# Decoder layer on one core: x1 turned by DVE instead of PE in the attending stage

## The reference

```python
x = _layernorm(x + _L0_attn_ref(x, L0_attn_w_qkv, L0_attn_w_out), axis=-1)
x = _layernorm(x + _L0_xattn_ref(x, ctx_1024, ctx_1024, mask, W_q, b_q, W_k, b_k, W_v, b_v, W_o, b_o), axis=-1)
x = _layernorm(x + _L0_ffn_ref(x, kernel, bias, a, b), axis=-1)
```

```python
q, k, v = split(queries @ W_q + b_q), split(keys @ W_k + b_k), split(values @ W_v + b_v)
scores = where(mask == 0, -1e6, einsum('bhqd,bhkd->bhqk', q, k) / sqrt(32))
out = einsum('bhqk,bhkd->bhqd', softmax(scores), v) @ W_o + b_o
```

## Time and profile before

| | us |
|---|---|
| runs | 956.74, 960.45, 960.53 |
| median | 960.45 |
| profiled execution | 956.11 |
| its span, first to last instruction | 954.3 |
| granted TensorE clock, mean over the span | 0.978 |

### The profile page before, as it was taken

How to read it: one execution, slowest core, us unless ns; L and a number is a source line. 1 busy time by engine, 2 the same in 40 slices (tenths; PEclk the granted TensorE clock), 3 DMA queues, 4 the chain that set the end, 5 groups by cost and what they waited for, 6 DMA issues and landing times.

```text
span 954.3 us, 14493 instructions
## 1 busy us (share of the span) xinstructions
PE 903.3 (95%) x4348; PEld 741.0 (78%) x4348; DVE 675.6 (71%) x1132; ACT 378.1 (40%) x1403; POOL 375.7 (39%) x338
## 2 busy tenths in 40 slices
PE   4897999999999999999779999999999999999997
PEld 4783887888888888888678788888888888888775
DVE  3364466666666657466668988979889798887967
ACT  3152221201020211101386656746467565675711
POOL 2000364334343534314237454344544354433733
PEclk9997999999999999999879999999999999999999
DMA  5965430415325120103513032220322204120021
GB/s 181 317 162 90 97 78 34 100 55 78 75 57 86 56 78 22 67 23 124 176 41 99 22 93 64 81 75 22 99 55 90 66 20 125 29 90 20 17 78 45
DMA packets 134172, 76.03 MB, mean 80 GB/s; under 512 B 104488, under 2 KB 106792, under 8 KB 134128
## 3 DMA queue, kind: packets, MB, share of 16 engines
q1 hardware_dynamic: 134127, 75.49, 29.4%
HBM read 52.60 MB, written 22.87 MB: 79 GB/s over the span
## 4 chain that ended last, share of the span: by engine, by line
PE 40%; DVE 5%; issue 2%; ACT 2%; POOL 2%; DVEq 0%; POOLq 0%
PE shared_ps L85 30%; PE score_ps L85 4%; PE shared_ps L1164 4%; ACT probs L1370 1%; DVE score_ps L1676 1%; PE shared_ps L1197 1%; PE shared_ps L1127 1%; POOL probs L1519 1%; DVE xT_lo L1633 1%; DVE x_and_res L1722 1%; DVE stats L1706 0%; DVE pT_lo L1660 0%; DVE top_s L1681 0%; DVE y L1700 0%; POOL x_and_res L1534 0%
## 5 line engine op out<-in xcount | busy, mean ns | idle before, releaser
L1370 ACT ACTIVATE probs<-score_ps,top_s 128x77 f32<-128x77 f32 x512 | 159.0, 359 | 37.7 <-DVE top_s L1681 37.4
L1370 ACT ACTIVATION_READ_ACCUMULATOR probs<-score_ps,top_s 128x1 f32 x512 | 123.1, 241 | 0.0
L1519 POOL TENSOR_TENSOR probs<-probs,per_total 128x616 f32<-128x616 f32 x64 | 82.7, 1308 | 66.0 <-DVE per_total L1688 65.8
L1512 POOL TENSOR_TENSOR rstd<-ve,half_power 128x1 f32<-128x1 f32 x64 | 42.3, 661 | 155.9 <-DVE ve L1711 151.4
L1676 DVE COPY_PREDICATED score_ps<-hidden,masked 128x616 f32<-128x616 int32 x64 | 66.6, 1040 | 11.3 <-PE score_ps L85 11.2
L1377 ACT ACTIVATE pT_hi<-shared_ps 103x512 fp32r<-103x512 f32 (+1 forms) x96 | 54.8, 612 | 44.0 <-PE shared_ps L1164 43.5
L723 POOL TENSOR_TENSOR vals<-qs_prod 128x512 f32<-128x512 f32 x32 | 41.1, 1294 | 69.4 <-DVE qs_prod L818 69.4
L707 POOL TENSOR_TENSOR xT_lo<-x_tok,xT_hi 128x512 fp32r<-128x512 f32 x28 | 38.0, 1361 | 76.5 <-ACT xT_hi L659 76.5
L672 ACT ACTIVATE qT_hi<-vals 128x512 fp32r<-128x512 f32 x32 | 19.4, 631 | 122.3 <-POOL vals L723 106.5
L714 POOL TENSOR_TENSOR mix_rstd<-mix_ve,half_power 128x1 f32<-128x1 f32 x32 | 22.1, 690 | 113.1 <-DVE mix_ve L837 113.1
L1660 DVE TENSOR_TENSOR pT_lo<-shared_ps,pT_hi 103x512 fp32r<-103x512 f32 (+1 forms) x96 | 64.5, 684 | 0.0
(11 more groups left out here) (210 smaller groups left out, 2691.8 us busy)
## 6 DMA issues: line engine op xcount, KB each, us to landing
x_tok<-in_x SPq DMA_DIRECT2D x32, 256.0 KB, 5.1
x_res<-in_x SPq DMA_DIRECT2D x8, 1024.0 KB, 7.0
x_between<-mix_x SPq DMA_DIRECT2D x32, 256.0 KB, 2.0
x<-x_between SPq DMA_DIRECT2D x8, 1024.0 KB, 5.6
x_tok<-x_between SPq DMA_DIRECT2D x8, 1024.0 KB, 5.7
out<-y_out SPq DMA_DIRECT2D x32, 256.0 KB, 2.0
wqkv_sb<-in_w_qkv SPq DMA_DIRECT2D x4, 768.0 KB, 7.6
keys_split<-w_q_hi SPq DMA_DIRECT2D x8, 154.0 KB, 5.6
```

The source lines that it names most:

```text
L1370: nc.scalar.activation(probs[:, t % 2, j * KEYS:(j + 1) * KEYS], score_ps[:, g, k * KEYS:(k + 1) * KEYS], ACT.Exp, bias=top[:, t % 2, j:j ...
L1512: nc.gpsimd.tensor_tensor(rstd[:, n:n + 1], ve[:, n:n + 1], half_power[:], ALU.pow).then_inc(rstd_ready, 1)
L1519: nc.gpsimd.tensor_tensor(p, p, per_total[:, t % 2, h * heads:(h + 1) * heads].unsqueeze(2) .to_broadcast([P, heads, KEYS]), ALU.mult).the ...
```

## The change

x1 of the next entry is loaded by `load_swapped`, DVE turns it (`turn_x1` moves from PE to DVE), ACT's `split_x1` reads it from the tile in place of a bank, and POOL makes the remainder (`rem_x1`), under the semaphores `x1_turned`, `x1T_hi` and `x1T_lo`. X disappears from the bank tables. The handover does the same, with the remainder on DVE. All the orders of the attending stage, of every engine and of the start, closing and end, are written anew; the counts of all other instructions stay. In a full step PE's list has its transposes in ten runs before, and in eight after.

```diff
@@ mix_tokens, SP, PE, ACT and DVE
-            sp.dma_start(x1_next[:], x1_dram[0].rearrange("(t p) d -> p t d", p=P)).then_inc(x1_loaded, 16)
+            load_swapped(sp, x1_next, x1_dram[0], x1_loaded)
...
-                if half == 0:
-                    pe.wait_ge(x1_loaded, 16)
-
-                    pe.wait_ge(kv_done, nth(B - 1, 8, 7))
-                    pe.wait_ge(qs_done, nth(B - 1, 8, 7))
-                    for c in range(NC):
-                        for t in range(NT):
-                            last = nc.tensor.transpose(next_banks[c][:, t * P:(t + 1) * P],
-                                                       x1_next[:, t, c * P:(c + 1) * P], ident[:])
-                        last.then_inc(hand.filled, 1)
...
+            dve.wait_ge(x1_loaded, SWAPPED)
+            dve.wait_ge(q_filled, nth(B - 2, 4, 3))
             for c in range(NC):
+                nc.vector.transpose(x1_next[:, c, :], x1_next[:, c, :]).then_inc(hand.x1_turned, 1)
+            for c in range(NC):
+                dve.wait_ge(hand.x1_turned, c + 1)
                 dve.wait_ge(hand.x1T_hi, c + 1)
-                nc.vector.tensor_tensor(x1T[1][:, c, :], next_banks[c][:], x1T[0][:, c, :].bitcast(F32),
-                                        ALU.subtract).then_inc(hand.freed, 1)
+                nc.vector.tensor_tensor(x1T[1][:, c, :], x1_next[:, c, :], x1T[0][:, c, :].bitcast(F32),
+                                        ALU.subtract).then_inc(hand.x1T_lo, 1)
@@ bank tables
-BACK, FRONT, NEXT = "VOTF", "P", "XQ"
+BACK, FRONT, NEXT = "VOTF", "P", "Q"
...
@@ attend, SP
                 wait_reuse(sp, x1T_hi, i * NC)
-                sp.dma_start(x1[:], x1_dram[i].rearrange("(t p) d -> p t d", p=P)).then_inc(x1_loaded, 16)
+                wait_reuse(sp, x1T_lo, i * NC)
+                load_swapped(sp, x1, x1_dram[i], x1_loaded)
@@ attend, PE
-            def turn_x1(i, s, c):
...
                 if c == 0:
                     pe.wait_ge(x1T_hi, nth(i, NC, NC - 1))
-
-                    pe.wait_ge(freed, s.emptied("X3"))
+                    pe.wait_ge(x1T_lo, nth(i, NC, NC - 1))
...
@@ attend, ACT
             def split_x1(i, s, c):
-                use = f"X{c}"
-                act.wait_ge(filled, s.filled(use))
-                nc.scalar.activation(x1T[0][:, c, :], shared_ps[s.bank(use)][:], ACT.Copy).then_inc(x1T_hi, 1)
+                if c == 0:
+
+                    act.wait_ge(filled, s.filled("O3") if "O3" in s.order else s.filled_before)
+                act.wait_ge(x1_turned, nth(i, NC, c))
+                nc.scalar.activation(x1T[0][:, c, :], x1[:, c, :], ACT.Copy).then_inc(x1T_hi, 1)
...
@@ attend, POOL
+            def rem_x1(i, s, c):
+                if c == 0:
+                    pool.wait_ge(filled, s.filled("O3") if "O3" in s.order else s.filled_before)
+                pool.wait_ge(x1_turned, nth(i, NC, c))
+                pool.wait_ge(x1T_hi, nth(i, NC, c))
+                nc.gpsimd.tensor_tensor(x1T[1][:, c, :], x1[:, c, :], x1T[0][:, c, :].bitcast(F32),
+                                        ALU.subtract).then_inc(x1T_lo, 1)
...
@@ attend, DVE
-            def split_x1(i, s, c):
-                remainder(s, f"X{c}", x1T_hi, nth(i, NC, c), x1T[0][:, c, :], x1T[1][:, c, :],
-                          shared_ps[s.bank(f"X{c}")][:])
+            def turn_x1(i, c):
+                if c == 0:
+                    dve.wait_ge(x1_loaded, (i + 1) * SWAPPED)
+                nc.vector.transpose(x1[:, c, :], x1[:, c, :]).then_inc(x1_turned, 1)
...
```

More of the change, by code:

```diff
@@ L691, in _ @@
             steps(act, step)
+            act.wait_ge(q_filled, nth(B - 2, 4, 3))
+            for c in range(NC):
+                act.wait_ge(hand.x1_turned, c + 1)
+                nc.scalar.activation(x1T[0][:, c, :], x1_next[:, c, :], ACT.Copy).then_inc(hand.x1T_hi, 1)
             for c in range(NC):
                 act.wait_ge(hand.filled, c + 1)
-                nc.scalar.activation(x1T[0][:, c, :], next_banks[c][:], ACT.Copy).then_inc(hand.x1T_hi, 1)
-            for c in range(NC):
-                act.wait_ge(hand.filled, NC + c + 1)
                 nc.scalar.activation(qT[0][:, c, :], next_banks[c][:], ACT.Identity,
@@ L1120, in _ @@
         def _(pe):
-            def turn_x1(i, s, c):
-                if c == 0:
-                    pe.wait_ge(x1_loaded, nth(i, 1, 0) * 16)
-                use = f"X{c}"
-                wait_reuse(pe, freed, s.reusable(use))
-                for t in range(NT):
-                    last = nc.tensor.transpose(shared_ps[s.bank(use)][:, t * P:(t + 1) * P],
-                                               x1[:, t, c * P:(c + 1) * P], ident[:])
-                last.then_inc(filled, 1)
             def project_q(i, s, c):
@@ L1449, in _ @@
             exponentials(0, 3, 0)
-            exponentials(0, 3, 1)
             split_q(1, s, 0)
             split_probs(0, s, 2, 0)
+            exponentials(0, 3, 1)
+            split_q(1, s, 1)
             split_probs(0, s, 2, 1)
-            split_q(1, s, 1)
-            split_probs(0, s, 2, 2)
             act.wait_ge(w_loaded[0], 16)
@@ L1458, in _ @@
             split_q(1, s, 2)
+            split_probs(0, s, 2, 2)
+            act.wait_ge(w_loaded[1], 16)
+            nc.scalar.activation(w_ffn[0][:], raw_ffn, ACT.Copy).then_inc(w_hi, 1)
             split_probs(0, s, 3, 0)
@@ L1461, in _ @@
             split_probs(0, s, 3, 2)
-            act.wait_ge(w_loaded[1], 16)
-            nc.scalar.activation(w_ffn[0][:], raw_ffn, ACT.Copy).then_inc(w_hi, 1)
             split_q(1, s, 3)
@@ L1540, in step @@
                 bias_residual(i - 1, 2)
+                normalize_probs(i, 0, 0)
+                root(i, s, "O0")
+                normalize_probs(i, 0, 1)
                 bias_residual(i - 1, 3)
-                normalize_probs(i, 0, 0)
-                normalize_probs(i, 0, 1)
-                root(i, s, "O0")
                 bias_x2(i, s, 0)
@@ L1591, in _ @@
             root(B - 1, s, "O1")
-            normalize_probs(B - 1, 1, 0)
-            normalize_probs(B - 1, 1, 1)
+            normalize_probs(B - 1, 2, 0)
+            root(B - 1, s, "O2")
+            normalize_probs(B - 1, 2, 1)
             bias_x2(B - 1, s, 1)
-            root(B - 1, s, "O2")
-            normalize_probs(B - 1, 2, 0)
-            normalize_probs(B - 1, 2, 1)
             bias_x2(B - 1, s, 2)
@@ L1600, in _ @@
             normalize_probs(B - 1, 3, 0)
+            root(B - 1, s, "O3")
             normalize_probs(B - 1, 3, 1)
-            root(B - 1, s, "O3")
             bias_x2(B - 1, s, 3)
@@ L1610, in _ @@
             bias_residual(B - 1, 1)
+            root(B, s, "O0")
             bias_residual(B - 1, 2)
+            root(B, s, "O1")
             bias_residual(B - 1, 3)
-            root(B, s, "O0")
             bias_x2(B, s, 0)
-            root(B, s, "O1")
-            bias_x2(B, s, 1)
             root(B, s, "O2")
             root(B, s, "O3")
+            bias_x2(B, s, 1)
+            root(B, s, "F0")
             bias_x2(B, s, 2)
-            root(B, s, "F0")
             bias_x2(B, s, 3)
@@ L1763, in step @@
+                normalize_o(i, s, 2)
+                split_probs(i, s, 0, 2)
+                add_o(i, s, 3)
+                turn_x1(i + 1, 3)
+                normalize_f(i, s, 0)
+                add_f(i, s, 1)
+                split_x2(i, s, 2)
                 split_probs(i, s, 1, 0)
-                measure(i, s, "F0")
+                softmax_top(i, 3, 0)
+                invert_totals(i, 2)
+                softmax_top(i, 3, 1)
                 split_probs(i, s, 1, 1)
-                split_x2(i, s, 1)
```

338 lines of the change are left out of this document (170 added, 168 removed).

## The result

The changed kernel takes 946.94 us in the median of four runs (944.34 to 949.12), the kernel before 958.6 in four (956.44 to 960.53). The ratio is 0.9878, with a 95% interval of 0.984 to 0.9916: 1.2% faster. The forecast was 945, the range 936 to 956. The profiled execution took 946.56 us, 9.55 less than the one before (956.11). The sum of the prediction was 13.8, so the total came nearer than its parts: one term of it had the wrong size by 5.6 us.

The account below looks back on a forecast made before the run. PE was taken to bound the repeated steps. Gains of 9.1 (steps 2 to 6), 2.7 (step 1), 0.5 (handover) and 1.5 (start) sum to 13.8 us: 956.1 to 942.3, plus some 3 for the median, 945; range 936 to 956.

Parts of the forecast that it names:

- PE's turns: Full step: sixteen turns of x1 leave PE, 1.63 us plus 0.19 for two fewer runs; 1.82 a step, 9.1 in five.
- The root of F0: POOL in a step: the root stands behind two x1 remainders and costs DVE about half a us, covered by slack.
- The recurring wait: Every step: PE waits 0.5 us for DVE's remainder of x2; the forecast counted it as staying.
- The x1 race: From O3's end in a step: ACT and POOL need 8.0 to 8.5 us, PE 9.1, so Q0 waits for nothing.
- Masked copies: DVE's copies against POOL's work: one 0.9 us collision more, one less, nothing on PE; at most two a step over 1.2.
- Handover: Handover stage: PE's 16 turns go, but PE stands still until POOL's remainder ends, a gap of about 1.1; 0.5 us gained.
- Start and step 1: Start stage 1.5 us gained; step 1 2.7 gained (bounds 1.8 and 3.6), with half the excess of its x2 wait.
- Closing and end: Last two stages: written in another order without a turn of x1; nothing gained (bounds 1.5 us either way).
- the second one: Rival: the recurring 0.5 us wait leaves every step and the start gives 4; 936 to 940 us, chance 0.15.
- the copies gave nothing back: Rival: the fourth tile's first masked copy waits 2.96 us; 11 of 13.8 us are lost, 953 to 957, chance 0.14.
- Q0 waited for nothing: Rival denied here: x1 comes 4.0 us late for Q0 in six steps and the start; 973 us, chance 0.07.
- x1 was there when DVE wanted it: Rival denied here: x1's load lands after DVE wants it and PE pays what it saved; 958 us, chance 0.04.

Follow-up runs that it names:

- POOL clear of O0: Changed kernel with POOL's second first-tile normalizing ahead of the root of O0 and its fourth residual add behind x2's first bias, in six full steps; 940.44 us.

## Why the prediction was right, and where it was not

**How near it came is in part luck.** The profiled execution was forecast at 942.3 us and took 946.56, because the sum was 4.2 too large. To that the forecast added some 3 us for the distance of the median from the profiled execution; this was 0.4. The two misses cancel to the 1.9 us between 945 and 946.94. The kernel before measured 958.6 beside the change and not 960.45, so the change won 11.7 us where the forecast stood for 15.5. The mechanism, PE as the bound of a step and its turns as the gain, is what was right.

**PE's turns: right.** The mechanism and the price of 0.10 us a turn were confirmed by the twelve added turns that lay on the path. 1.82 us a step were forecast and 1.67 measured. The missing 0.15 is less than what the stall ahead of F2 costs: with the root of F0 in front, a step is 56.92, that is 1.93 below before.

**The root of F0: mis-sized.** The prediction had it stand behind two remainders and cost DVE half a us, covered by DVE's slack. It cost DVE 1.21 us, because POOL also stands 2.07 us for ACT ahead of the first remainder, and 0.26 us of it reached PE. The slack of 8.8 us was no cover: the turns added on DVE show that 5.6 us more of its work cost 3.87. Cover is what lies ahead of the next thing that PE takes from DVE, and not the sum of DVE's idle time. For the four turns of x1 themselves no run shows a cost in a step: with POOL clear of O0 they stand where they stood, and PE's list of waits in steps 2 to 6 is empty.

**The recurring wait.** It was counted as staying, and one of that size stayed (0.65 for 0.50), but from another place: POOL's second normalizing on top of DVE's normalizing of O0. Its removal is worth 0.80 us a step. This was to be read in the order, where the root of O0 stands directly ahead of the second half, and in the trace of the kernel before, whose own recurring wait stands behind the same collision:

```profile
591.93 2.58 POOL L1519 TENSOR_TENSOR probs<-probs,per_total 128x616 f32<-128x616 f32 x2 [0.20 <-DVE per_total L1688]
592.52 0.91 DVE L1722 TENSOR_SCALAR x_and_res<-y,mv,rstd 128x512 f32<-128x512 f32 x1
593.36 0.68 DVE L1633 TENSOR_TENSOR xT_lo<-shared_ps,xT_hi 128x512 fp32r<-128x512 f32 x1
594.09 0.50 PE L85 MATMUL shared_ps<-w_ffn_hi,xT_hi 128*128 128x512 f32 x1 [0.50 <-DVE xT_lo L1633]
```

The normalizing takes 0.91 us beside POOL's and not 0.54, the remainder stands behind it, and PE waits 0.50 us for the remainder. That these 0.37 us are the larger part of the wait is read from the rows; no run tested it.

**The x1 race: right, but narrower.** POOL's last remainder ran from 717.48 for 2.09 us, where 1.30 was forecast, and ended at 719.57, and Q0 started at 720.13: won by 0.56 us, just under the 0.6 to 1.1 forecast.

**Masked copies: right.** At most two long ones a step were forecast, there is one, and PE's waits in steps 2 to 6 name none of them.

**Handover: right.** PE's gap ahead of the second half of the projection was forecast at 1.1 us and measured at 0.97:

```profile
448.70 0.50 PE L632 MATMUL out_ps<-w_back_hi,qT_hi 128*128 128x512 f32 x1 [0.97 <-POOL qT_lo L725]
445.36 2.49 DVE L884 STREAM_TRANSPOSE x<-x 128x512 f32<-128x512 f32 x4 [1.84 <-DMA x<-x_between]
```

DVE's turns wait 1.84 us for the swapped load, which lands at about 445 as estimated, and nobody waits for them.

**Start and step 1.** -1.24 for -1.5, and -3.30 for -2.7. The start's size is not settled: in the nine experiments, which all have the changed kernel's start, it took 40.9 to 43.7 us, in one of them longer than before, and before only one profile shows it (42.49).

**Closing and end: the step that failed.** "Nothing (bounds 1.5 either way)" was set because no x1 is turned there. Their orders were written anew all the same. The closing gained 2.15 us and the end lost 5.62, of which the experiments put 3.9 to the order of roots, residual adds and normalizings, 1.7 to the clock and nothing to the late load. The closing's gain was not taken apart, but it is no accident of one execution: from its first weighing to that of the end the closing took 48.41 us before, 46.35 in the changed kernel and 46.33 to 46.37 in all nine experiments. Without the end's term the measured sum would have been 9.6 + 5.6 = 15.2 us against 13.8.

**The rivals.** What the second one counts on, that the recurring wait goes too, was there to be had (0.80 us a step), but not by this change as it is: the old one went and a new one came. The others left no trace: the copies gave nothing back, Q0 waited for nothing, and in the steps x1 was there when DVE wanted it.

## What to carry to other kernels

Where a change writes orders anew, read every stage that it touches, also those without the operation that it is about: 3.9 us were lost in the one that was priced at nothing. On an engine that runs others' small links (a root, a reciprocal), put the link ahead of long work that waits for something, and put long work that nobody waits for where the receiver of the link isn't just starting. Price an engine's idle time by what stands ahead of the next consumer, not by its sum.

## What the runs showed of the hardware

A normalizing on DVE (one 128x512 tile in SBUF with two scalars for each partition, into SBUF) takes 0.54 us, and in the changed kernel 1.33 to 1.43 when a POOL operation on SBUF tiles of 1.22 to 1.29 us has started up to 0.17 us ahead of it. In the kernel before, two of them in a full step took 0.91 to 1.12, met later in POOL's operation. The prediction had priced only the masked copies against POOL. The Trainium skill, "SBUF — State Buffer", section Who interferes with whom, lists such a tensor-by-scalar operation among those that can take the port pair shared with GpSimd, when its operands meet the conditions of a two-port mode, and says that in such a mode whoever issues first gets the pair for the whole instruction. The rows agree: the operation that began at 697.48 ended at 698.81, 0.28 us behind POOL's at 698.53, and with POOL's work moved away it took 0.55. The other way round, the normalizing at 711.58 started 0.18 us ahead of POOL's remainder at 711.76: it took 0.54, and the remainder 1.52 in place of some 1.3. In which mode the operation ran no row shows.

The granted clock can fall to 1.2 GHz inside a product that follows a wait of 1.77 us: O0 of the end took 4.41 to 4.42 us in four of the profiled executions, 4.30 in one, and 2.80 to 2.85 in the six others, behind the same wait of 1.76 to 1.77. What decides it was not found.
